# Forming step size times u on VectorE instead of GpSimd in a Mamba stage

## The reference

```python
xs = silu(conv(xs) + convb)                    # called u in the kernel
dt = softplus(dt @ dtW.T + dtb)                # called delta, the step size
dA = exp(dt[..., None] * A)
dBx = dt[..., None] * Bm[:, :, None, :] * xs[..., None]
h = h * dA_t + dBx_t                           # over the positions, for each state
y = einsum('bds,bs->bd', h, C_t)
y = (y + xs * Dskip) * silu(z)
```

## Time and profile before

| | |
|---|---|
| median of 3 runs | 2175.49 us (2172.94 to 2176.54) |
| profiled execution | 2173.8 us, its span 2172.0 us |
| busy in the span | TensorE 86%, VectorE 82%, ScalarE 63%, GpSimd 60% |
| mean granted clock of TensorE | 0.924 of full |

### The profile page before, as it was taken

The page is one execution under the profiler, slowest core; times in us unless marked ns, Lnnn a source line. Parts: engine busy times, 40 slices in busy tenths (PEclk is TensorE's granted clock), DMA queues, the critical chain, the costliest instruction groups (busy, mean ns, idle before and its releaser), DMA issues. The chain is left out here.

```text
span 2172.0 us, 32672 instructions
## 1 busy us (share of the span) xinstructions
PE 1866.3 (86%) x10276; PEld 993.4 (46%) x10276; DVE 1787.1 (82%) x2181; ACT 1378.2 (63%) x2602; POOL 1295.0 (60%) x954
## 2 busy tenths in 40 slices
PE   5898989887989898779888499996689999999987
PEld 5333333333333333234565278884234555565532
DVE  6599899999898999978877899996977666667683
ACT  3666666767676767448335477773167877777776
POOL 4789899999898999952134255544662111111276
PEclk7999999999989999899998799996589999999999
DMA  3345454455445455532003000001334334333212
GB/s 81 110 154 153 148 155 158 155 157 160 147 153 153 154 153 155 160 104 71 31 1 95 0 1 0 0 0 59 93 87 121 94 111 118 99 112 111 74 39 79
DMA packets 156310, 217.53 MB, mean 100 GB/s; under 512 B 31722, under 2 KB 68603, under 8 KB 155547
## 3 DMA queue, kind: packets, MB, share of 16 engines
q1 hardware_dynamic: 152074, 207.41, 31.5%
q0 software_dynamic: 4096, 8.40, 1.5%
HBM read 196.59 MB, written 23.86 MB: 101 GB/s over the span
## 5 line engine op out<-in xcount | busy, mean ns | idle before, releaser
L1035 POOL TENSOR_TENSOR m_dBx<-m_du,m_rowB 128x1024 f32<-128x1024 f32 x256 | 605.0, 2389 | 4.7 <-DMA m_rowB<-bc_rows 4.5
L758 PE MATMUL ps<-m_hC,ident 128*128 128x512 f32 x1024 | 512.8, 647 | 99.2 <-DVE m_hC L1117 99.2
L3225 DVE TENSOR_REDUCE a_mx<-ps 128x2 f32<-128x1024 f32 (+2 forms) x320 | 344.6, 1114 | 100.7 <-PE ps L2799 55.8
L934 ACT ACTIVATE ps<-m_delta,m_A 128x512 f32<-128x512 f32 x512 | 332.7, 682 | 143.7 <-DVE m_hC L1117 112.8
L3017 ACT ACTIVATE a_pT<-ps 128x512 f32<-128x512 f32 (+2 forms) x640 | 318.0, 563 | 135.0 <-PE ps L2827 116.9
L758 PEld LDWEIGHTS ps<-m_hC,ident 128*128 128x128 f32 x1024 | 203.6, 206 | 391.8 <-issue 231.4
L3381 POOL TENSOR_SCALAR_AFFINE_SELECT a_pT<-a_pT 128x512 f32<-128x512 f32 x104 | 66.0, 637 | 372.0 <-ACT a_pT L3017 370.6
L1117 DVE TENSOR_TENSOR m_hC<-ps,m_rowC 128x1024 f32<-128x1024 f32 x176 | 215.3, 1223 | 16.7 <-issue 1.3
L1108 DVE TENSOR_TENSOR_SCAN ps<-ps,m_dBx 128x1024 f32<-128x1024 f32 x88 | 201.1, 2285 | 33.3 <-ACT ps L934 16.7
L1045 POOL TENSOR_TENSOR m_hC<-m_h,m_rowC 128x1024 f32<-128x1024 f32 x80 | 194.6, 2432 | 45.5 <-DVE m_h L1108 45.3
L1108 DVE TENSOR_TENSOR_SCAN ps<-ps,m_carry,m_dBx 128x1024 f32<-128x1024 f32 x88 | 206.3, 2345 | 5.5 <-ACT m_dBx L959 4.6
(11 more groups left out here) (410 smaller groups left out, 3618.6 us busy)
## 6 DMA issues: line engine op xcount, KB each, us to landing
m_rowB<-bc_rows SPq DMA_DIRECT2D x256, 256.0 KB, 4.0
m_rowC<-bc_rows SPq DMA_DIRECT2D x256, 256.0 KB, 3.4
a_w<-in_L3f_w1T SPq DMA_DIRECT2D x39, 256.0 KB, 2.7
a_w<-in_L3f_w2T SPq DMA_DIRECT2D x39, 256.0 KB, 3.8
expert_rows<-in_zero_rows SPq DMA_DIRECT2D x39, 128.0 KB, 2.6
a_xs<-expert_rows SPq DMA_DIRECT2D x39, 128.0 KB, 2.6
expert_out<-a_y SPq DMA_DIRECT2D x39, 128.0 KB, 3.6
qk_parts<-a_part SPq DMA_DIRECT2D x18, 256.0 KB
```

The source lines that it names most:

```text
L758: mm = pe.matmul(ps[:, bankY + c, :], k.ident[:], hC[:, n % NBUF, c, :], start=False, stop=n % NS == NS - 1)
L934: act.activation(decays(n)[:, c, :], delta[:, i % 2, c, chunk(i, x)], ACT.Exp, scale=An[:, ITEMS[i][0], c, s:s + 1]).then_inc(decayed, 1)
L1035: pool.tensor_tensor(dBx[:, n % NBUF], du[:, i % 2, :, chunk(i, x)], rowB[:, n % 4, :].unsqueeze(1).to_broadcast([P, HALF, CH]), ALU.mult) ...
L3225: dve.tensor_reduce(mx[:, c % 2, :, es[0]:es[0] + len(es), t, x // CH], src, AX_X, ALU.max)\
```

## The change

VectorE forms du, for each half right behind the addition that completes its delta, at n = 6 for the second half of item 0 and at q = 25 and 26 for the next item. It waits for that addition by its semaphore, as the two read and write the same tile. GpSimd keeps only the overwriting of the column, at the same places of its order as before, and waits for du before it. Those who waited for GpSimd's du now wait for VectorE's.

```diff
-        V_PREP = Marks(k, "m_dve_prep", ["delta0", "delta1"])
-        G_PREP = Marks(k, "m_pool_prep", ["du0", "reset0", "du1", "reset1"])
+        V_PREP = Marks(k, "m_dve_prep", ["delta0", "du0", "delta1", "du1"])
+        G_PREP = Marks(k, "m_pool_prep", ["reset0", "reset1"])
...
                         if c == 0 and t == 0 and i >= 2:
-                            act.wait_ge(G_PREP.sem, G_PREP.at("du1", i - 2))
+                            act.wait_ge(V_PREP.sem, V_PREP.at("du1", i - 2))
...
-                def inputs(i, x):
-
-                    cols = chunk(i, x)
-                    pool.wait_ge(V_PREP.sem, V_PREP.at(f"delta{x}", i))
-                    if x == 0 and i >= 2:
-                        pool.wait_ge(dbx, step(i - 1, 0, 0))
-                    G_PREP.done(pool.tensor_tensor(du[:, i % 2, :, cols], delta[:, i % 2, :, cols], u[:, i % 2, :, cols],
-                                                   ALU.mult), f"du{x}", i)
-                    pool.wait_ge(G_PREP.sem, G_PREP.at(f"du{x}", i))
+                def reset(i, x):
+
+                    pool.wait_ge(V_PREP.sem, V_PREP.at(f"du{x}", i))
                     if x == 1:
                         pool.wait_ge(A_SECOND.sem, A_SECOND.at("decay", i))
...
                     if s == 0:
-                        pool.wait_ge(G_PREP.sem, G_PREP.at(f"du{x}", i))
+                        pool.wait_ge(V_PREP.sem, V_PREP.at(f"du{x}", i))
...
                     if q == 12:
-                        inputs(i, 1)
+                        reset(i, 1)
                     if q == 29 and i + 1 < N:
-                        inputs(i + 1, 0)
+                        reset(i + 1, 0)
...
+                def inputs(i, x):
+
+                    cols = chunk(i, x)
+                    dve.wait_ge(V_PREP.sem, V_PREP.at(f"delta{x}", i))
+                    if x == 0 and i >= 2:
+                        dve.wait_ge(dbx, step(i - 1, 0, 0))
+                    V_PREP.done(dve.tensor_tensor(du[:, i % 2, :, cols], delta[:, i % 2, :, cols], u[:, i % 2, :, cols],
+                                                  ALU.mult), f"du{x}", i)
...
                 add_soft(0, 0)
+                inputs(0, 0)
...
                     if n == 6:
                         add_soft(0, 1)
+                        inputs(0, 1)
                     if q in (25, 26) and i + 1 < N:
-                        add_soft(i + 1, q - 25)
+                        add_soft(i + 1, (25, 26).index(q))
+                        inputs(i + 1, (25, 26).index(q))
```

More of the change, by code:

```diff
@@ L1023, in inputs @@
                     g, _, begin, _ = ends(i)
-                    column = cols.start + begin
+                    column = chunk(i, x).start + begin
                     G_PREP.done(pool.memset(delta[:, i % 2, g, column:column + 1], RESET), f"reset{x}", i)
@@ L1050, in _ @@
                     G_FRONT.done(add_normalized(k, pool, E, g), f"res{g}")
-                inputs(0, 0)
+                reset(0, 0)
                 for n in range(NST):
```

## The result

The changed kernel takes 2220.43 us (median of 4 runs, 2216.16 to 2224.32) against 2174.22 before (4 runs): 46.2 us more. The ratio is 1.0198 with the 95% interval 1.017 to 1.0226; the quotient of the two medians, 1.0213, lies inside it. The forecast was 2223, +47.8. The profiled execution took 2216.16 us, its span 2214.4.

What follows compares the result with a forecast made beforehand. VectorE was taken to bound the Mamba stage, with GpSimd close behind. Fifteen blocked du at 3.26 us (+48.9) less 1.1 at the start gave +47.8 us, forecast 2223 us (own range 2218 to 2229; overall 2208 to 2241).

Steps and rivals of the forecast that it cites:

- VectorE sets the pace, GpSimd has room: Mamba stage: work added to VectorE is paid for; the 37.6 us GpSimd saves becomes waiting for scans, gaining nothing.
- 15 du at 3.26: Behind the additions at steps 25, 26 and item 0's step 6: each du blocked by a GpSimd operation, +48.9 us.
- No du went free: Rival: one du of each two goes free as GpSimd waits for a scan or row; 13.7 less, 2210 us; chance 0.10.
- Why GpSimd gets in: Between addition and du: du's own wait makes it ask 0.25 us after GpSimd's next operation has begun.
- The rule of the Trainium skill that was a rival: Between addition and du: a free semaphore leaves GpSimd no gap; +15.7, 2191 us; within the du-length rival, chance 0.07.
- The first one gains 1.1: Stage start, GpSimd idle: the first du is not blocked and everything behind it comes 1.1 us earlier.
- The second addition keeps winning: Second addition, seven items: probably gets in before GpSimd again; rival, it is blocked too, 16 more, 2239 us, chance 0.08.
- TensorE's clock: Head of an item: clock goes with step 8's wait, 4.48 or 2.78 us; uncertainty 5.1 us either way.
- du by its length alone: Rival: du is not blocked and costs only 1.3 us each, 15 x 1.3 - 1.1 = +18.4, 2194 us; chance 0.07.
- GpSimd as the pace: Rival: GpSimd's queue bounds the stage, so its 37.6 us saving comes off, 2138 us; chance 0.03.

Runs made afterwards that it cites:

- giveway: The changed kernel with three added GpSimd waits for du, before operations that had slipped in between addition and du: 2188.66 us.
- opp_q11: Kernel before, GpSimd keeping du and also taking the half-1 additions before its weighing at q = 11; overwrite and ScalarE decay moved: 2166.87 us.
- probe_tiny2: Kernel before plus 15 VectorE products of 128x2 constants in SBUF, each behind an addition and waiting for it as du does: 2210.41 us.
- probe_one1024: Kernel before plus 15 VectorE sums over 1024 columns of a weight tile (one SBUF input), in du's places with du's wait: 2198.28 us.
- adjacent: Changed kernel with half-0 du behind scan 26, second addition directly behind it without a wait, half-1 du behind scan 27 (item 0: 7): 2215.3 us.
- firstdu: Kernel before with only the very first du (item 0, half 0) on VectorE, GpSimd waiting for it and forming the others: 2175.09 us.
- spread: Changed kernel with additions behind scans 25 and 27, du behind scans 26 and 28 (item 0: behind 7): 2209.49 us.
- probe_one: Kernel before plus 15 VectorE sums over a 512-column weight tile (one SBUF input), in du's places with du's wait: 2197.16 us.
- first_giveway: Kernel before with the first du on VectorE, and GpSimd waiting for item 0's second addition before its product of step 8: 2172.99 us.

## Why the prediction was right, step by step

- *VectorE sets the pace, GpSimd has room.* Right. GpSimd's saved work became waiting, `giveway` put waits on GpSimd at no visible cost, and `opp_q11` gained by moving work to it.
- *15 du at 3.26.* Right: mean 3.243 in the rows, 6.56 per pair. No du went free: the shortest of the 15 took 3.24. The price is 1.2 of length and 2.0 of standing behind GpSimd; `probe_tiny2` shows the second part with almost no length, `probe_one1024` the first without the second, `giveway` takes the second away. The Trainium skill, SBUF — State Buffer, section Who interferes with whom, says that a VectorE instruction with two SBUF inputs contends with a GpSimd one that reads SBUF, and that one with at most one SBUF input, outside the 2-port perf modes, does not. The 3.24 of du and the 1.22 of the sum in `probe_one1024` agree.
- *Why GpSimd gets in.* Only partly right. I put it down to the gap of 0.25 us that du's own wait leaves. `adjacent` shows it without that wait. The gap was also smaller than I took it: the 0.09 us behind the shown end were read from a weighing behind a scan, but du starts 0.03 behind the addition's shown end (169.85 against 168.55 + 1.27 = 169.82). The wait is thus 0.11 in du's place, not 0.17. The price did not move, as it counts from GpSimd's start. The rule of the Trainium skill that was a rival (VectorE: DVE Perf Modes, The DRAIN you can't avoid: a semaphore costs nothing extra) would not have saved du even if it held. The rows do not bear it out: 0.03 after the end with a wait, 0.08 before it without.
- *The first one gains 1.1.* Right in the trace (5.04 against 6.19 us, and 5.15 in `firstdu`), though no time shows it alone.
- *The second addition keeps winning.* Right, 1.20 in all seven items of the changed kernel; but only by its moment: in `probe_one1024`, where it asked 1.3 us after that GpSimd product's row began (170.81 against 169.54) and not 0.03, it took 2.15.
- *TensorE's clock.* The term that moved. At step 8, VectorE's timeline after, items 1 and 5:

```profile
226.18 2.30 DVE L1111 TENSOR_TENSOR_SCAN ps<-ps,m_dBx 128x1024 f32<-128x1024 f32 x1 [2.79 <-ACT ps L934]
693.96 2.30 DVE L1111 TENSOR_TENSOR_SCAN ps<-ps,m_dBx 128x1024 f32<-128x1024 f32 x1 [4.48 <-POOL m_dBx L1029]
```

Five of six waits are now the short ones, one long, where it was three and three: 3.4 us less, within the 5.1 allowed. That these waits go with the clock holds throughout. The busy time of the five us that begin 1 us after the start of the gate at the head of the item, for the two rows above, clock third from last:

```profile
202.07:207.07 5.00, 4.63 (x13) 2.27 (x14) 4.91 (x4) 3.26 (x7) 2.45 (x2) 1.00 0.36 102
668.16:673.16 5.00, 4.64 (x7) 2.03 (x8) 4.91 (x4) 3.45 (x7) 2.59 (x3) 0.66 0.29 108
```

The twelve profiles hold 72 such waits. In that stretch the granted clock was 0.66 to 0.68 before each of the 28 long ones and 1.00 before each of the 44 short ones. Why an item falls on one side or the other isn't known: `probe_tiny2` had six long ones, `opp_q11` none.

A second wait I had not seen: 2.71 us at step 4 of item 0 in the kernel before, gone after. VectorE's row before:

```profile
93.49 2.30 DVE L1108 TENSOR_TENSOR_SCAN ps<-ps,m_dBx 128x1024 f32<-128x1024 f32 x1 [2.71 <-ACT ps L934]
```

The busy time of 80 to 85 us, before and then after:

```profile
80.00:85.00 5.00, 3.85 (x5) 0.90 (x6) 3.95 (x4) 4.87 (x9) 5.00 (x3) 0.53 0.36 122
```

```profile
80.00:85.00 5.00, 5.00 (x12) 1.60 (x11) 4.00 (x3) 4.87 (x10) 5.00 (x3) 1.00 0.37 118
```

TensorE was granted 0.53 of its clock there, close to its lower level of 1.2 GHz, and after the change 1.00, 2.4 GHz. The other profiles agree: the wait is 2.58 at 0.50 (`opp_q11`), 1.16 to 1.44 in the six with 0.66 to 0.70 (`probe_tiny2` 1.35, `giveway` 1.43), and gone in `probe_one1024`, `spread` and `firstdu`, all at 1.00. As `probe_one1024` has nothing of the change at its start, I don't count it to the change.

For the profiled pair the sum is then 48.9 - 1.1 - 3.4 - 2.7 = +41.7 against 2216.2 - 2173.8 = +42.4 measured. Of these 42.4, 40.9 lie between the stage's first addition and the start of its last gate (892.9 to 933.8 us), 0.6 ahead of it and 0.9 behind it. The medians give +46.2 for the forecast +47.8. Whether the two waits level out over their executions isn't shown, as only one of each kernel was profiled; some of this closeness may be luck.

The rivals: du by its length alone (2194) is what `giveway` made of it (2188.7, with the addition at step 6 of item 0 freed as well), not what the change did. GpSimd as the pace is refuted.

## What to carry to other kernels

Moving an elementwise product with two SBUF inputs to VectorE, next to a GpSimd that works without pause, costs its length plus what is left of GpSimd's operation, whatever its size, and sometimes more (next section): look in the trace for VectorE rows of the same shape with two durations (here 1.20 and 3.41) before pricing it. If it must be there, let GpSimd wait for it at that place, or set it where GpSimd stands idle. And where VectorE has no idle time, look for GpSimd's waits and move work into them.

## What I had not expected of the hardware

A VectorE operation that stands blocked is not always let in at the end of the GpSimd operation that blocks it. The addition at step 6 of item 0 took 1.2 to 3.4 us in seven of the profiled kernels, in two of which GpSimd waits for it, but 8.06, 8.77 and 9.03 in three others (`firstdu`, `adjacent`, `probe_one`). GpSimd runs several operations back to back there in the kernels without such a wait, the quick ones included. In `adjacent`, VectorE and then GpSimd:

```profile
98.72 8.77 DVE L1076 TENSOR_TENSOR m_delta<-m_delta,m_soft 128x1024 f32<-128x1024 f32 x1
```

```profile
97.14 2.37 POOL L1039 TENSOR_TENSOR m_hC<-m_h,m_rowC 128x1024 f32<-128x1024 f32 x1
99.45 6.97 POOL L1029 TENSOR_TENSOR m_dBx<-m_du,m_rowB 128x1024 f32<-128x1024 f32 x3
```

The addition asked in the middle of the first and was done only when all four were through. In the changed kernel it asked at 98.46, 0.12 us after such an operation had begun, and took 3.33; in `probe_tiny2` it asked 1.52 after one had begun, as in `adjacent` (1.58), and took 1.92. What decides who is next stays open; `first_giveway`, in which GpSimd waits there, had 1.87.

No scan was blocked. Between 80 and 900 us every scan of the twelve profiles took 2.27 to 2.36 us beside GpSimd, though it reads dBx, and in the second half the carried state, from SBUF. Its decays lie in PSUM.
